# A cross-attention and mixture-of-experts kernel: five queues reordered, and two inverse deviations computed on ScalarE and VectorE instead of GpSimd

## The reference

```python
x = x + tanh(g_xattn[0]) * attention(layernorm(x), ctx, Wq, bq, Wk, bk, Wv, bv, Wo, bo)
x = x + tanh(g_ffn[0])   * moe(layernorm(x), router_w, w_in, b_in, w_out, b_out)

def moe(x, ...):
    logits = x @ router_w                      # 8 experts
    top_p, top_e = top_k(softmax(logits), 2)
    h = gelu(x[pair] @ w_in[e] + b_in[e])      # 2 pairs for each token
    y = (h @ w_out[e] + b_out[e]) * top_p
    out[token] += y
```

## Time and profile before

| | us |
|---|---|
| median of 3 runs | 276.29 (276.13 to 279.11) |
| the profiled execution's own time | 275.26 |
| its span | 273.4 |
| PE busy | 237.6 (87%) |
| DVE, POOL, ACT busy | 166.2, 143.6, 134.9 |
| 46 slot tiles, from the first transpose to the last scatter | 155.9 to 260.7 |

### The profile page before, as it was taken

The page is one execution under the profiler, slowest core; times in us unless marked ns, Lnnn a source line. Parts: engine busy times, 40 slices in busy tenths (PEclk is TensorE's granted clock), DMA queues, the critical chain, the costliest instruction groups (busy, mean ns, idle before and its releaser), DMA issues.

```text
span 273.4 us, 5539 instructions
## 1 busy us (share of the span) xinstructions
PE 237.6 (87%) x1644; PEld 187.0 (68%) x1644; DVE 166.2 (61%) x512; ACT 134.9 (49%) x306; POOL 143.6 (53%) x181
## 2 busy tenths in 40 slices
PE   7899989995699999989688689999999999999900
PEld 4575543653367465734576489999999999999800
DVE  3897957973286548669658026585435343457745
ACT  4347444711771873165314055666566665656520
POOL 3689327327875760003867754444477774446520
PEclk9999999999799999999889979999999999999985
DMA  7910950292233010000222555534353373797365
GB/s 211 340 53 4 448 185 7 78 324 83 77 115 115 17 63 0 2 0 35 82 78 78 154 162 164 161 115 119 118 170 115 106 212 119 223 363 264 116 204 181
DMA packets 25837, 37.34 MB, mean 137 GB/s; under 512 B 3497, under 2 KB 22954, under 8 KB 25714
## 3 DMA queue, kind: packets, MB, share of 16 engines
q1 hardware_dynamic: 21074, 19.91, 24.2%
q0 software_dynamic: 3744, 10.24, 10.4%
q10 hardware_dynamic: 992, 6.84, 7.3%
HBM read 24.64 MB, written 18.39 MB: 157 GB/s over the span
## 4 chain that ended last, share of the span: by engine, by line
PE 48%; POOL 14%; DVE 12%; issue 11%; DMA 10%; ACT 3%; ACTq 0%; POOLq 0%; SPq 0%; DVEq 0%
PE pA L1293 10%; PE pG L1293 9%; PE pM L1293 9%; POOL y_rows L603 8%; DMA stage<-in_w_out 4%; PE pM L1361 4%; PE pA L1622 2%; PE pA L1413 2%; POOL slots L595 2%; PE pA L1399 2%; PE pA L1654 2%; ACT prob L692 2%; PE pA L1419 2%; DVE st L875 2%; POOL rstd L491 2%
## 5 line engine op out<-in xcount | busy, mean ns | idle before, releaser
L603 POOL DMA_INDIRECT y_rows<-y_sb,dst_i x46 | 46.0, 1000 | 40.2 <-ACT y_sb L838 35.9
L1233 DVE TENSOR_TENSOR hT_lo<-pA,hT_hi 128x256 fp32r<-128x256 f32 x46 | 19.5, 424 | 44.3 <-ACT hT_hi L832 44.1
L919 DVE TENSOR_REDUCE mx<-pM 128x4 f32<-128x308 f32 x64 | 27.6, 471 | 21.5 <-PE pM L1361 20.8
L595 POOL DMA_INDIRECT slots<-z2a,pos_u x16 | 16.0, 998 | 29.9 <-DVE pos_u L1133 25.7
L825 ACT ACTIVATE h_sb<-pM 128x256 f32<-128x256 f32 x46 | 17.6, 383 | 23.2 <-PE pM L1293 23.2
L1293 PE MATMUL pM<-win_hi,xT_hi 128*128 x92 | 26.6, 289 | 0.0
L1293 PE MATMUL pM<-win_lo,xT_hi 128*128 x92 | 26.5, 288 | 0.0
L1293 PE MATMUL pM<-win_hi,xT_lo 128*128 x92 | 26.4, 287 | 0.0
L1293 PE MATMUL pA<-wout_hi,hT_lo 128*128 x92 | 25.9, 282 | 0.0
L1293 PE MATMUL pA<-wout_lo,hT_hi 128*128 x92 | 25.9, 281 | 0.0
L1293 PE MATMUL pA<-wout_hi,hT_hi 128*128 x92 | 25.9, 281 | 0.0
(11 more groups left out here) (255 smaller groups left out, 657.1 us busy)
## 6 DMA issues: line engine op xcount, KB each, us to landing
xg<-slots SPq DMA_DIRECT2D x46, 128.5 KB, 2.4
slots<-in_empty ACTq DMA_DIRECT2D x1, 3983.5 KB, 14.8
x_sb<-in_x SPq DMA_DIRECT2D x4, 512.0 KB, 7.1
stage<-in_w_in SPq DMA_DIRECT2D x8, 256.0 KB, 2.7
stage<-in_w_out SPq DMA_DIRECT2D x8, 256.0 KB, 2.6
slots<-in_empty ACTq DMA_DIRECT2D x1, 1927.5 KB, 8.0
yc<-y_rows SPq DMA_DIRECT2D x6, 256.0 KB, 4.5
out<-x_sb SPq DMA_DIRECT2D x6, 256.0 KB, 2.2
```

The costliest lines, as they stand in the source:

```text
L595: pool.indirect_dma_start(out=slots[GROUP[s]], out_offset=bass.IndirectOffsetOnAxis(ap=pos_u[:, s, q:q + 1], axis=0), in_=z2[int(s > 0)][: ...
L603: pool.indirect_dma_start(out=y_rows[int(j >= JB)], out_offset=bass.IndirectOffsetOnAxis(ap=dst_i[:, j:j + 1], axis=0), in_=y_sb[:, j % YR ...
L919: nc.vector.tensor_reduce(dst[:, 2 * g:2 * g + 2, 2 * h:2 * h + 2], pM[:, g, 0:4 * KV].rearrange("p (r s n) -> p r s n", s=2, n=KV), AX_X, ...
L1233: nc.vector.tensor_tensor(hT_lo[:, j % 2, :], pS[:, 1, 0:D], hT_hi[:, j % 2, :].bitcast(F32), ALU.subtract).then_inc(h_lo, 1)
```

## The change

Each engine's program has some of its steps in another order; the inverse deviations of the second layernorm of blocks 2 and 3 are computed as Exp(-0.5 * Ln(var + eps)) on ACT and refined by one Newton step on DVE, where POOL had computed them between its sends; and five `keep_busy` matmuls are added.

```diff
@@ PSUM bank of ranks(0)
-        pR = [pG, pS, pG]
+        pR = [pM, pS, pG]
@@ POOL
-            split_weights(0, 4)
+            split_weights(0, 2)
             inv_std(0, 3, var1, rstd1)
             inv_std(1, 0, var2, rstd2)
-            split_weights(4, 12)
+            split_weights(2, 12)
             inv_std(1, 1, var2, rstd2)
@@ POOL, send_stage
                     send(s, 0, t)
-                    if s == 0 and t == 2:
-                        inv_std(1, 2, var2, rstd2)
...
                         send(s, 1, t)
-                        if s == 0 and t == 1:
-                            inv_std(1, 3, var2, rstd2)
@@ ACT
+            def inverse_std(b):
+
+                act.wait_ge(var2, b + 1)
+                nc.scalar.activation(rstd[:, 1, :], veps[:, 1, :], ACT.Ln).then_inc(ln_step, 1)
+                act.wait_ge(ln_step, b - 1)
+                nc.scalar.activation(rstd[:, 1, :], rstd[:, 1, :], ACT.Exp, scale=-0.5).then_inc(std_ready, 1)
...
                 split_q(b + 1, 0)
-                if b == 1:
-                    norm2(0)
...
                 exp(b, 4)
                 exp(b, 5)
+                if b == 1:
+                    norm2(0)
                 if b:
                     split_c(b, 0)
                 invert(b, 1)
...
             split_c(3, 0)
+            inverse_std(2)
             split_c(3, 1)
             norm2(2)
             copy_z2(2)
+            inverse_std(3)
             norm2(3)
             copy_z2(3)
@@ DVE
+            def stats2_ln(b):       # stats2, but its last instruction writes var + eps instead of -mean
...
+                nc.vector.tensor_scalar(veps[:, 1, :], mv[:, 1, :, 1], EPS, None, ALU.add).then_inc(var2, 1)
+
+            def refine_std(b):
+
+                r = rstd[:, 1, :]
+                dve.wait_ge(std_ready, b - 1)
+                dve.wait_ge(z2_ready, b)
+                link(nc.vector.tensor_tensor(nm[:, 1, :], r, r, ALU.mult))
+                link(nc.vector.tensor_tensor(nm[:, 1, :], nm[:, 1, :], veps[:, 1, :], ALU.mult))
+                link(nc.vector.tensor_scalar(nm[:, 1, :], nm[:, 1, :], -0.5, 1.5, ALU.mult, ALU.add))
+                link(nc.vector.tensor_tensor(r, r, nm[:, 1, :], ALU.mult))
+                nc.vector.scalar_tensor_tensor(out=nb[:, 1, :], in0=mv[:, 1, :, 0], scalar=-1.0, in1=r,
+                                               op0=ALU.mult, op1=ALU.mult).then_inc(rstd2, 1)
...
-            residual(2)
             choose(0, 0)
             choose(0, 1)
             count_first()
             place_pairs(0)
+            residual(2)
             refine(3, 0)
             normalise_attention(3, 0)
-            stats2(2)
+            stats2_ln(2)
             refine(3, 1)
             normalise_attention(3, 1)
+            refine_std(2)
             split_c(3, 0)
             split_c(3, 1)
             experts(0)
             residual(3)
-            stats2(3)
+            stats2_ln(3)
             take_logits(2)
+            refine_std(3)
             choose(1, 0)
@@ PE, project(3, 1)
-                        pe.wait_ge(rank_taken, 1)
                         pe.wait_ge(x1_ready, 3)
@@ PE, ranks(0)
                 if n == 0:
-                    pe.wait_ge(x1_ready, 3)
+                    pe.wait_ge(sm_red, 16 * BLOCKS)
@@ PE
             scores(3, 0)
+            ranks(0)
             scores_rest(3, 0)
             denominators(3, 0)
+            pe.wait_ge(rank_taken, 1)
             scores(3, 1)
-            ranks(0)
...
             transpose_x(0)
+            keep_busy(pA[:, 3, :], w_hi[0], 3)
             transpose_x(1)
+            keep_busy(pA[:, 3, :], w_hi[0], 2)
```

More of the change, by code:

```diff
@@ L300, in build @@
         var1, var2, rstd1, rstd2 = sem("var1"), sem("var2"), sem("rstd1"), sem("rstd2")
+        ln_step, std_ready = sem("ln_step"), sem("std_ready")
         z_ready, zT_ps, z_hi, z_lo = sem("z_ready"), sem("zT_ps"), sem("z_hi"), sem("z_lo")
@@ L956, in stats2 @@
                 stats(1, xs(b), var2)
+            def stats2_ln(b):
+                dve.wait_ge(x1_ready, b + 1)
+                dve.wait_ge(rstd2, b)
+                for i in range(BLK):
+                    last = nc.vector.bn_stats(st6[:, 1, i, :], xs(b)[:, i, :])
+                link(last)
+                for i in range(BLK):
+                    last = nc.vector.bn_aggr(mv[:, 1, i, :], st6[:, 1, i, :])
+                link(last)
+                nc.vector.tensor_scalar(veps[:, 1, :], mv[:, 1, :, 1], EPS, None, ALU.add).then_inc(var2, 1)
[9 more added lines that the diff above has]
+                                               op0=ALU.mult, op1=ALU.mult).then_inc(rstd2, 1)
             def take_logits(b):
```

## The result

| | before | changed |
|---|---|---|
| median of 4 runs, us | 277.45 (276.13 to 279.11) | 268.05 (266.63 to 272.15) |
| the profiled execution's own time | 275.26 | 266.63 |
| its span | 273.4 | 264.8 |
| PE, DVE, ACT, POOL busy | 237.6, 166.2, 134.9, 143.6 | 235.4, 168.1, 135.3, 140.3 |

The ratio is 0.9649 with a 95% interval of 0.9574 to 0.9723 (it leaves out disturbed runs, which is why it isn't the quotient of the medians). The profiled execution became 8.6 us shorter and the median 9.4; 7.35 were forecast.

What follows compares the result with a forecast made beforehand. PE, nearly always busy from 160 us, was taken to bound the kernel, so its slot tiles' start counts. 5.7 + 0.35 + 1.3 = 7.35 off the profiled 275.26 gives 267.9, or 268.9 as median; range 267.3 to 270.3, 8 in 10: 266 to 272.8.

Steps and rivals of the forecast that it cites:

- A: Block 1: POOL's inverse deviations earlier and norm2(0) behind exp(1, 5) let exp(1, 3) start earlier; 5.7 us gained.
- B: Block 3: earlier ranking and sends, but PE's queue, delayed by refine_std and choose(1), sets the end; 0.35 us gained.
- C: First slot tiles: dense filler and five added keep_busy matmuls keep the clock from falling at 159; 1.3 us gained.
- POOL's late splits: POOL's eight splits 4 to 11 end about 85.2, rstd2 for block 1 at 86.8; slack 1.7 us, costed at nothing.
- the clock rival: PE's longer wait ahead of ranks(1) lowers the clock in block 3's logits or at the first tiles: 270.4; chance 0.20.
- VectorE beside POOL: Block 1's second half: POOL's splits stretch two of VectorE's cT_lo splits on the path, costing 0.9: 269.8; chance 0.08.
- Late splits: POOL's splits delay rstd2 for block 1, holding up ACT at norm2(1): up to 275, chance 0.08; beyond 279, 0.04.
- The early sends do count: Start of slot tiles: with PE's queue shorter than forecast, the 7.9 us of POOL's path come out in part: 264; chance 0.04.
- The order not felt: Block 1: something unseen holds exp(1, 3) until 69, leaving only B and C: 274.6; chance 0.04.

Runs made afterwards that it cites:

- after_again: The changed kernel once more, unaltered, as reference for the second job; ratio to the kernel before 0.970, median 267.26 us.
- a_both: The kernel before with POOL's inverse deviations ahead of matrices 2 and 3 and norm2(0) behind exp(1, 5), nothing else; ratio 0.980, median 269.83 us.
- a_pool: The kernel before with POOL's new order alone, norm2(0) staying ahead of exp(1, 3); ratio 0.976, median 269.09 us.
- a_norm: The kernel before with norm2(0) moved behind exp(1, 5) alone, POOL keeping its order; ratio 0.976, median 268.86 us.
- pool_inv: The changed kernel with inverse deviations of blocks 2 and 3 back on POOL between sends, no Ln, Exp or Newton step; 265.34 us, ratio to before 0.962.
- pool_no16: The changed kernel without the 16 keep_busy behind logits(3), inverse deviations of blocks 2 and 3 on POOL; 265.78 us, ratio to before 0.964.
- no_five: The changed kernel without the five keep_busy matmuls at the first two transposes; 268.33 us, ratio to before 0.973.
- best: The changed kernel without 16 keep_busy behind logits(3), refine_std(2) behind VectorE's splits, 15 fillers for 8 before ranks(1), HOLD 13; 261.59 us, ratio to before 0.952.

## Why the prediction was right

The absolute forecast was 268.9, the median 268.05. As a ratio it had 0.973, just outside the measured 0.957 to 0.972: the gain was forecast too small, 7.35 us against 8.6 by the profiled executions and 9.4 by the medians, and the median of the kernel before came out 1.2 above the one that the forecast started from. Divided by place:

| us gained | forecast | changed | after_again |
|---|---|---|---|
| A, up to scores(3, 0) | 5.7 | 5.8 | 6.4 |
| B, from there to the first tile | 0.35 | 1.0 | -0.3 |
| C, from there to the first `second` | 1.3 | 1.1 | 1.1 |
| from there to the end of the span | 0 | 0.6 | 0.8 |

*Part A, 5.7 us.* Right in its mechanism and its size. The pieces: scores(3, 0) at 109.38 (109.6 forecast), exp(1, 3) at 65.23 (65.1), rstd2 at 62.3 (62.1), 1.24 us back from the clock (1.3), norm2 hidden. a_both, a_pool and a_norm (0.976 to 0.980) show that it is the cause of some two thirds of the whole. What the prediction did not see is that one of the two edits would have been enough. Its account of ACT's queue held all that was needed for it: with POOL early, norm2 would have fitted between 63.2 and 65.3.

*POOL's late splits, costed at nothing.* The eight splits ended at 86.0 (85.2 forecast) and rstd2 came at 87.6 (86.8), 0.7 ahead of its reader at 88.4 (88.5). The 85.2 doesn't follow from the 66.0 ahead of it: 18.4 us for the eight, as before, would end at 84.4. In the trace the two loaded splits ended at 66.2, POOL then waited 1.75 us for the next load, and started at 67.9. The cover was there, at less than half the size of the forecast 1.7.

*Part B, 0.35 us.* The right number is partly luck. The mechanism is right in this: the path is PE's queue and not the sends (pool_inv and pool_no16 show both sides), project(3, 1) came 0.65 later behind scores(3, 0) than before (0.6), pos_u at 116.5 (116.6), the last send at 136.87 (137). The Ln and the Exp took 0.20 and 0.21 where 0.25 was taken, and the Newton step 0.98 for 1.0. The figure of the Trainium skill, "ScalarE: Activation LUTs", section "What ACT_TABLE_LOAD costs", 0.19 for four columns, was the nearer one; so was a row of the kernel before that the prediction passed over, 0.193 for an ACTIVATE of 128x2 (`tg<-gates_in`). The step that failed is the clock, at two places. The prediction kept the low level in project(3, 1), since it came after a wait of 2.36 before; in the changed kernel a wait of 3.05 stood there and nothing fell. And it kept the full clock behind ranks(1), where the wait grew from 1.09 to 1.93: there the level was low at 141 to 144.4, as the clock rival had it, to which it gave 0.20. In the changed kernel's execution the two errors nearly cancel. after_again, the same program, had the low level at both places: 12.80 us from project(3, 1) to ranks(1) where the changed kernel took 11.44, and B came to -0.3 instead of 1.0.

The two places are not alike. Behind ranks(1) the six executions with a wait of 1.84 to 1.93 all fell and the six with 1.09 to 1.11 did not: the rival's condition held every time, at a price of 0.9 (8.99 us from ranks(1) to the first tile against 8.06 in pool_inv) where it had 1.3 to 1.7. At project(3, 1) the level differed from execution to execution, and that belonged into the forecast as an uncertainty of B of 1.4 us.

*Part C, 1.3 us.* No low level at the first tiles, as forecast. From the first tile to the first `second` it took 7.66 instead of 8.80, 1.1 us. But no_five shows that the five fillers are not what holds the clock, and dense filler stood ahead of the first tile before as well, with 1.80 us of waiting for the rows between. What changed is that wait. (A filler is 3.92 / 16 = 0.245 us by its row, not 0.22; three of them still fit in 1.02.)

*What was left over.* From the first `second` to the end of the span the changed kernel took 108.1 us and the one before 108.7; across all fourteen executions that stretch lies between 107.5 and 109.4. The 0.6 are within what this stretch does by itself.

*The rivals.* The clock falls elsewhere: it did, behind ranks(1), in both executions of the changed kernel; the 270.4 of that rival didn't come, not even with low levels at both places (after_again, 267.39). VectorE beside POOL: a cT_lo split took 1.18 us at 71.17, so the stretching is real, but it was off the path. Late splits: no. The early sends do count, in the form that PE's queue is shorter than forecast: no; pool_no16 shows when they would. The order not felt: no.

## What to carry to other kernels

When two queues meet at one point, find which of them has filler in it: a faster partner is worth nothing before the filler goes, and an edit that speeds up one path by lengthening the other has to be weighed again once it is gone. A wait that an operation imposes on what stands behind it can be cured at either end, by making its input earlier or by moving it back; count the gain once. And before the granted clock of a stretch is built on, read several executions: at one place here it differed from one to the next, at two others it was the same each time and went with the wait ahead of it.

## What the runs showed of the hardware

What PE waited ahead of three places, in the fourteen profiled executions, and in how many of them the granted clock was at 0.50 within 4 us behind it:

| place | wait of PE, us | executions | of them with the low level |
|---|---|---|---|
| project(3, 1) | 2.31 to 2.38 | 8 | 4 |
| project(3, 1) | 3.02 to 3.05 | 6 | 5 |
| ranks(1) | 1.84 to 1.93 | 6 | 6 |
| ranks(1) | 1.09 to 1.11 | 6 | 0 |
| ranks(1) | 0.55 or none | 2 | 0 |
| first tile, for the rows | 1.67 to 3.28 | 5 | 5 |
| first tile, no wait for the rows | | 9 | 0 |

So the length of a single wait doesn't decide it from place to place: after 2.32 us of waiting the clock stayed at 1.00 (best, at project(3, 1)), after 3.05 too (changed), and after the same 3.05 in after_again, the same program, it was down at once. Each fall lasted 3.3 to 3.5 us, or about twice that. What else decides it was not tried.

An inverse deviation of 128x4 costs 1.6 us on POOL with its two neighbours, of which 1.04 for the power; by Ln, Exp and a Newton step it is 0.2 + 0.2 on ACT and 1.0 on VectorE, in three engines' queues instead of one.
